# Attention images in DRAM: four slots per row in place of six, and each 48-row stack in two loads of 24 rows

## The reference

```
h = layer_norm(x, ln1_w, ln1_b)
q = (h @ Wq + bq).reshape(B, L, N_HEADS, HEAD_DIM)
k = (h @ Wk + bk).reshape(B, L, N_HEADS, HEAD_DIM)
scores = jnp.einsum('blhd,bmhd->bhlm', q, k) * scale + bias
attn = jax.nn.softmax(scores, axis=-1)
ctx = jnp.einsum('bhlm,bmhd->blhd', attn, v)
```

## Time and profile before

| what | value |
|---|---|
| median of 3 runs | 2529.16 us (2527.45 to 2529.85) |
| the profiled execution, its own time | 2526.43 us |
| its span, first to last instruction | 2524.7 us |
| PE busy | 2101.1 us (83%) |
| VectorE busy | 1811.5 us (72%) |
| ScalarE busy | 1619.7 us (64%) |
| queue of SP: packets, MB, share of 16 DMA engines | 82400, 102.99, 18.9% |
| HBM written | 42.40 MB |

### The profile page before, as it was taken

The page is one execution under the profiler, slowest core; times in us unless marked ns, Lnnn a source line. Parts: engine busy times, 40 slices in busy tenths (PEclk is TensorE's granted clock), DMA queues, the critical chain, the costliest instruction groups (busy, mean ns, idle before and its releaser), DMA issues. The chain is left out here.

```text
span 2524.7 us, 44078 instructions
## 1 busy us (share of the span) xinstructions
PE 2101.1 (83%) x15464; PEld 902.6 (36%) x15464; DVE 1811.5 (72%) x4863; ACT 1619.7 (64%) x2370; POOL 517.2 (20%) x797
## 2 busy tenths in 40 slices
PE   6496488778377799999999987947999999999696
PEld 2375255556155222222222236721222222222375
DVE  7733595442585799999999925378999999996443
ACT  3043355333244479999999973434999999999443
POOL 6175220156111000000000014720000000000065
PEclk9598599889589689999999998965999999999798
DMA  2312560311570511111111011116011011010212
GB/s 66 94 48 70 82 120 5 94 36 49 94 136 11 142 28 22 23 30 22 23 30 22 9 54 51 52 38 154 15 30 30 16 30 30 15 30 2 73 47 86
DMA packets 94265, 127.17 MB, mean 50 GB/s; under 512 B 20762, under 2 KB 72448, under 8 KB 94048
## 3 DMA queue, kind: packets, MB, share of 16 engines
q1 hardware_dynamic: 82400, 102.99, 18.9%
q0 software_dynamic: 11648, 21.36, 2.9%
HBM read 79.88 MB, written 42.40 MB: 48 GB/s over the span
## 5 line engine op out<-in xcount | busy, mean ns | idle before, releaser
L1339 DVE TENSOR_REDUCE pair_mx<-ps 128x1 f32<-128x512 f32 x1520 | 959.0, 683 | 70.5 <-PE ps L1149 68.8
L1299 ACT ACTIVATE prob<-ps 128x1024 f32<-128x1024 f32 x1024 | 986.8, 1026 | 33.5 <-PE ps L1184 18.9
L1149 PE MATMUL ps<-k_stack,q_stack 48*128 48x512 bf16 x2048 | 572.8, 402 | 31.0 <-PEq L910 13.4
L1198 PE MATMUL ps<-prob,v_head 128*32 128x512 f32 x4096 | 547.0, 606 | 1.6 <-ACT prob L1299 1.0
L1184 PE MATMUL ps<-q_stack,k_stack 51*128 51x512 bf16 x2048 | 447.7, 383 | 12.6 <-ACT prob L1299 10.3
L1149 PEld LDWEIGHTS ps<-k_stack,q_stack 48*128 48x128 bf16 x2048 | 149.4, 94 | 500.7 <-DVE pair_mx L1339 342.3
L2214 DVE TENSOR_TENSOR hid<-silu,ps 128x256 f32<-128x256 f32 (+1 forms) x190 | 87.8, 463 | 246.2 <-PE ps L2067 164.2
L1691 DVE CUSTOM_DVE_ANT_0 ps<-ps,mask 128x256 f32<-128x256 f32 (+2 forms) x512 | 179.7, 418 | 46.2 <-PE ps L1495 43.9
L1273 ACT ACTIVATE qk<-ps 128x512 f32<-128x512 f32 x264 | 157.6, 597 | 80.9 <-PE ps L1149 65.8
L1184 PEld LDWEIGHTS ps<-q_stack,k_stack 51*128 51x128 bf16 x2048 | 102.4, 93 | 295.8 <-ACT prob L1299 253.4
L2067 PE MATMUL ps<-weight_raw,block 128*128 x632 | 193.5, 430 | 0.0
(11 more groups left out here) (249 smaller groups left out, 2292.0 us busy)
## 6 DMA issues: line engine op xcount, KB each, us to landing
q_stack<-image_dram SPq DMA_DIRECT2D x88, 192.0 KB, 4.5
k_stack<-k_wide_dram SPq DMA_DIRECT2D x60, 240.0 KB, 5.4
arena<-e_rows SPq DMA_DIRECT2D x32, 256.0 KB, 4.6
k_stack<-image_dram SPq DMA_DIRECT2D x32, 192.0 KB, 4.4
image_dram<-parts SPq DMA_DIRECT2D x30, 192.0 KB, 5.3
image_dram<-parts SPq DMA_DIRECT2D x30, 128.0 KB, 5.0
k_wide_dram<-parts SPq DMA_DIRECT2D x2, 1800.0 KB, 17.4
weight_raw<-in_L_ffn_Wg_dram SPq DMA_DIRECT2D x6, 528.0 KB, 5.0
```

Source lines behind the costliest of these rows:

```text
L1149: nc.tensor.matmul(max_bank(n), rows_of(c.q_stack, b, g, ROWS, slice(t * P, (t + 1) * P)), rows_of(c.k_rows, b, g, ROWS, slice(k * CHUNK, ...
L1198: ins = nc.tensor.matmul(out, c.v_head[:, e % 2, kb, :], unit, start=(kb == 0), stop=(kb == TILES - 1), skip_group_check=True)
L1299: nc.scalar.activation(c.prob[:, u % P_UNITS, :], c.ps[:, 2 * (u % 2) * CHUNK:2 * (u % 2) * CHUNK + UNIT], ACT.Exp, scale=scale).then_inc( ...
L1339: ins = nc.vector.reduce_max(mx[:, w:w + 1], max_bank(n), AX.X)
```

## The change

The image keeps four slots: queries P0 P1 P2 P1, keys P2 P1 P0 P0. The three parts of queries go to 1, 2 and 1 slots in place of 3, 2 and 1, those of keys to 2, 1 and 1 in place of 3, 2 and 1. A load becomes two, each of three slots, 24 rows: the first takes slots 0 to 2 (for queries slot 0 three times), the second slots 1 to 3. The rows of the stack come in another order, and the same six products are formed. The number of stores stays, that of loads doubles, and the waits count eight in place of four.

```diff
--- before.py
+++ after.py
@@ -48,13 +48,15 @@
 SLOTS = 6
+IMAGE_SLOTS = 4
+TRIO = SLOTS // 2
 ROWS = SLOTS * HD
...
-Q_SLOTS = (slice(0, 3), slice(3, 6, 2), slice(4, 5))
-K_SLOTS = (slice(2, 5), slice(1, 6, 4), slice(0, 1))
+Q_SLOTS = (slice(0, 1), slice(1, 4, 2), slice(2, 3))
+K_SLOTS = (slice(2, 4), slice(1, 2), slice(0, 1))
@@ -836,11 +838,22 @@
+def load_trios(engine, image, n, stack, head, b, g, cols, loaded):
+
+    rows = slice(head * HD, (head + 1) * HD)
+    for trio in range(2):
+        if trio == 0 and n == 0:
+            src = image[rows, 0:1, cols].broadcast_to((HD, TRIO, cols.stop - cols.start))
+        else:
+            src = image[rows, trio:trio + TRIO, cols]
+        at = g * HALF + trio * TRIO * HD
+        dst = stack[at:at + TRIO * HD, b, cols]
+        engine.dma_start(dst, src).then_inc(loaded.sem, 16)
+
+
 def load_piece(engine, c, n, head, b, g, cols, loaded):
 
-    rows = image_of(c, n)[head * HD:(head + 1) * HD, :, cols].rearrange("d s n -> (d s) n")
-    stack = (c.q_stack, c.k_rows)[n]
-    engine.dma_start(stack_rows(stack, b, g, ROWS, cols), rows).then_inc(loaded.sem, 16)
+    load_trios(engine, image_of(c, n), n, (c.q_stack, c.k_rows)[n], head, b, g, cols, loaded)
@@ -874,7 +887,7 @@
 def first_loads(n, paired):
 
-    return 4 if n == 0 or n == 1 and not paired else 2
+    return 8 if n == 0 or n == 1 and not paired else 4
@@ -1053,7 +1066,7 @@
-    LOADS = 4
+    LOADS = 8
@@ -1202,8 +1215,7 @@
         for n, (stack, cols) in enumerate(((c.q_stack, WHOLE), (c.k_rows, WIDE_KEYS))):
-            rows = image_of(c, n)[h * HD:(h + 1) * HD].rearrange("d s n -> (d s) n")
-            engine.dma_start(rows_of(stack, b, g, ROWS, cols), rows).then_inc(stack_loaded[b].sem, 16)
+            load_trios(engine, image_of(c, n), n, stack, h, b, g, cols, stack_loaded[b])
@@ -1572,8 +1584,7 @@
         for n, stack in enumerate((c.q_stack, c.k_stack)):
-            rows = c.image_dram[n, head * HD:(head + 1) * HD].rearrange("d s n -> (d s) n")
-            engine.dma_start(rows_of(stack, b, g, ROWS, slice(0, N_TOK)), rows).then_inc(stack_loaded[b].sem, 16)
+            load_trios(engine, c.image_dram[n], n, stack, head, b, g, WHOLE, stack_loaded[b])
@@ -2445,8 +2456,8 @@
-        c.image_dram = nc.dram_tensor("image_dram", (2, D, SLOTS, N_TOK), bf16).ap()
-        c.k_wide_dram = nc.dram_tensor("k_wide_dram", (D, SLOTS, N_TOK + CHUNK), bf16).ap()
+        c.image_dram = nc.dram_tensor("image_dram", (2, D, IMAGE_SLOTS, N_TOK), bf16).ap()
+        c.k_wide_dram = nc.dram_tensor("k_wide_dram", (D, IMAGE_SLOTS, N_TOK + CHUNK), bf16).ap()
```

## The result

The change made the kernel slower: 2545.99 us as the median of four runs (2544.23 to 2551.04), against 2529.51 us for the kernel before (2527.45 to 2530.21). The ratio on record is 1.008, 95% interval 1.0065 to 1.0095; the two medians alone are 16.5 us apart, a ratio of 1.0065. The forecast was 2518.0 us, and the range ended at 2529.

What follows compares the result with a forecast made beforehand. In the stretch before the second pair, the stores' bytes and then the loads on SP's queue were taken as the bound. Window stages 7.8 plus full stages 3.4 gave 11.2 us: 2529.16 to 2518.0 us, range 2514 to 2529.

Steps and rivals of the forecast that it cites:

- Loads: Step on SP's stack loads: each becomes two 24-row loads, issued in 0.345 us and moved in 0.56 us each.
- Stores: First window stage: two pairs' twelve stores fall from 24 units of 64 KB to 16, 15.1 us to 10.1.
- Loads, moving: How long a 24-row load moves: on eight engines, 0.56 us, with bounds 0.45 and 1.12 us.
- The second rival: Stack loads: eight engines move them at half rate, 1.12 us each; sum +5.8 us, 2535.0 us; chance 0.13.
- the third rival's: Words in the loads step for the sum if eight engines don't keep up; the rival so numbered had absorbed gains, chance 0.07.
- The 0.4 and 0.6 us: Full stages: the gains that remain if eight engines move loads at half rate.
- its own 4.5 us: Half-rate case: how much longer eight loads last when each moves in 1.12 us.
- 879.2: First full stage: forecast time at which the second head's stack is ready, from loads starting at 871.0 plus issues and lag.
- 884.72: First full stage, kernel before: time from which its 2.76 us wait is subtracted, giving 882.0, when TensorE wants the second head's stack.
- The sum, window stages: Two window stages: last second-pair load issued by 298.8, not 302.68; TensorE starts pair 1 3.9 us earlier, 7.8 us in all.
- The sum, full stages: Two full stages: second head's stack waits of 2.76 and 3.67 us go; VectorE regains 1.25 and 2.17 us, 3.4 in all.
- my 3.4: Full stages: the total gain in us, VectorE's 1.25 and 2.17, if the freed time runs to the stage's end.

Runs made afterwards that it cites:

- run 3: Kernel before (six slots, old stores) with each stack in two loads of 24 rows in a row, four dims by six slots: 2541.15 us, ratio 1.0055.
- run 2: Kernel before with only four of the six slots stored, one 48-row load per stack kept: 2503.55 us, ratio 0.9909.
- run 6: The change, but each half-load reads six dims of four slots, 24 rows in a row (sides matched): 2521.11 us, ratio 0.9976.
- run 5: run 3's kernel with later query loads of twelve dims by two slots, sides differing, key loads still matched: 2524.58 us, a single run.
- run 7: The change with the image by head, slot, dim, two matched 24-row loads, four stores per pair and operand, computing the whole: 2576.74 us, ratio 1.0201.
- run 8: run 7's image with one 48-row load of overlapping windows per stack, two for queries, three for keys: 2732.61 us, ratio 1.0815.

## Why the prediction was wrong

**The step that failed** is the price of a 24-row load's issue in "Loads". I took 0.345 us from an 8-row store and set the bounds at 0.30 and 0.46. It measured 0.65, and 0.694 from one to the next: twice my value and outside both bounds. I had let the number of rows and engines choose the nearest row. What both of my rows had in common, and the new load doesn't have, is that their two sides are alike. The kernel before has a transfer on SP whose sides differ, the shift store: 48 rows of the source go to three rows of the stack, cut in 16 pieces. In the earlier trace rows it stands at 326.31 with 0.76 us. It differs in size and in its pieces too, but it was the one row that hinted at the price, and I read it only for its time of day. For a 24-row load with matched sides my bounds would have held: run 3 has 0.365, 0.41 from one to the next.

**Stores:** right in what they move. In the window stage the twelve stores and the first two load issues behind them took 10.4 us (293.35 to 303.71) where I had 10.1 for the stores' 16 units; in run 2, where the loads are the old ones, it took 9.6 (284.01 to 293.58). In the first full stage the big stores, with their landing, took 17.5 us (868.84 to 886.35), from 26.1 before; 18.1 follows from my sum. That a two-slot store could itself be dear to issue (0.69 us in place of 0.30, the rows under run 6) I had not asked.

**Loads, moving:** eight small packets a load, as forecast. The eight engines kept up at the pace at which SP issued; how fast they would be at a cheaper issue stays open. The second rival, slower by half-rate engines, had the sign but not the mechanism; it is the one that I mean where I write "the third rival's". The 0.4 and 0.6 us that it leaves the full stages don't follow from its own 4.5 us: 879.2 + 4.5 is 883.7, still 1.0 us before the 884.72 of before, and the other stage gives 1.2.

**The sum, window stages:** the working nearly holds if 0.694 is put in. Eight first loads take 5.7 us (278.15 to 283.88) in place of my 2.8, and the six query stores behind them 3.4 in place of 2.8, so the next block begins at 287.69, 3.5 us later than before, where I had 0.2 earlier; 0.8 of it, as said above, was there before. Eight more take 5.7 again, and the last load of the second pair is issued by 307.87 in place of 298.8. At 0.365, run 6, the heads of the two window stages are 4.6 and 3.9 us shorter than before; I had said 3.9 each.

**The sum, full stages:** twelve early loads took 8.4 us (860.44 to 868.84), not 4.1, so the second head's loads came 886.35 - 860.44 = 25.9 us into the block, where they had come 28.8 after it began before (848.85 to 877.61). The waits went from 2.76 and 3.67 to 2.26 and 2.44 us, not to nothing. Where the loads are cheap they do go: runs 2 and 6 have no stack wait there. Run 2, with one load, then has 2.9 us less in the heads of the two stages, near my 3.4; run 6, with two, has 1.5.

**What I had left out:** the projection blocks of the full stages. The price of their first loads, and of the dear query stores, lies on the way to the block's end; I had costed only the loads, and only in the window stages. The blocks grew by 4.2 and 4.0 us in the change, and by 1.5 and 1.2 even in run 6. So with matched sides, too, the total is -5.7 us and not -11.2.

## What to carry to other kernels

In these runs the price of issuing a transfer depended on whether its two sides have the same shape, and not on its rows or bytes alone; so cost a new transfer by the row whose pair of shapes is most like it, and if a layout can make both sides plain rows at one step, choose that layout for the stores as well as the loads. When one transfer becomes two on a queue that has to issue in order, put the issue price on everything that stands behind them, the end of the block included. A layout also decides how many engines move a transfer: look at the outermost dimension of both sides before an image is turned round.

## What the runs showed of the hardware that was not expected

- The issue time on SP by the shapes of the two sides: 48 rows alike 0.42 us, 24 rows alike 0.365, 8 rows alike 0.30; 16 by 3 against 48 rows 0.59; 8 by 3 against 24 rows 0.65; 12 by 2 against 24 rows 0.77. With unlike sides fewer rows were no cheaper.
- An 8-row store to slots 1 and 3 of four took 0.69 us, to one slot or to two neighbouring ones of the keys 0.30 (the changed kernel).
- An issue with matched sides right behind one with unlike sides took 0.53 us, the next 0.36 (run 5).
- Sixteen 16-row stores cut as 2 by 8, on two engines, held the queue for 0.97 us per 64 KB on average, up to 1.32, where 16 plain rows hold it 0.63 (run 7). Two and three engines moved a head's four loads at some 50 to 80 GB/s (run 8), where sixteen reached 175.
